# The last three steps of two attention layers, finished amid the weighing of the following step

## The reference: what is computed

```python
h = jnp.maximum(_layernorm(x, axis=-1), 0.0)
x = x + layer(h, adj, ...)
```

```python
Wh = jnp.einsum('nf,hfo->hno', node_features, W)
e = leaky_relu(f_src[:, :, None] + f_dst[:, None, :], 0.2)
attn = jax.nn.softmax(jnp.where(adj > 0, e, NEG_INF), axis=-1)
h_prime = jnp.einsum('hnm,hmo->hno', attn, Wh)
```

## Time and profile before

| | |
|---|---|
| median of three runs | 1111.23 us |
| the profiled execution, its own time | 1109.11 us |
| its span, first to last instruction | 1106.9 us |
| TensorE matmul busy | 844.4 us (76%) |
| VectorE busy | 774.2 us (70%) |
| ScalarE busy | 430.3 us (39%) |
| GpSimd busy | 634.1 us (57%) |
| mean granted TensorE clock | 0.906 |

### The profile page before, as it was taken

The page is one execution under the profiler, slowest core; times in us unless marked ns, Lnnn a source line. Parts: engine busy times, 40 slices in busy tenths (PEclk is TensorE's granted clock), DMA queues, the critical chain, the costliest instruction groups (busy, mean ns, idle before and its releaser), DMA issues. The chain is left out here.

```text
span 1106.9 us, 11271 instructions
## 1 busy us (share of the span) xinstructions
PE 844.4 (76%) x2786; PEld 471.1 (43%) x2786; DVE 774.2 (70%) x2327; ACT 430.3 (39%) x1277; POOL 634.1 (57%) x636
## 2 busy tenths in 40 slices
PE   0889869999928745959999989467799928876354
PEld 0344434433317534835666646244444523332121
DVE  3899986943349839938689995477899825646374
ACT  3677868111115423624554334355663511110000
POOL 5003401667767777437776730677777057777772
PEclk9999989999959986988999999898999959997767
DMA  9998998938878898647887841678778267776761
GB/s 358 413 395 336 386 393 251 324 104 267 267 248 285 284 233 284 202 153 214 246 245 209 227 128 47 177 232 239 222 211 229 72 155 205 203 206 196 199 189 73
DMA packets 87599, 257.49 MB, mean 233 GB/s; under 512 B 18694, under 2 KB 22182, under 8 KB 83433
## 3 DMA queue, kind: packets, MB, share of 16 engines
q0 software_dynamic: 46896, 157.18, 49.3%
q1 hardware_dynamic: 33116, 85.89, 21.1%
q10 hardware_dynamic: 7516, 13.63, 3.5%
HBM read 209.81 MB, written 53.66 MB: 238 GB/s over the span
## 5 line engine op out<-in xcount | busy, mean ns | idle before, releaser
L1148 POOL DMA_INDIRECT arena<-T,arena x476 | 497.7, 1046 | 266.5 <-issue 202.8
L771 PE MATMUL psum<-arena,misc 128*128 128x512 f32 x408 | 207.3, 630 | 32.9 <-DVE arena L1527 25.4
L747 PE MATMUL psum<-arena 128*128 128x264 f32 (+1 forms) x832 | 207.8, 394 | 0.9 <-ACT arena L869 0.9
L670 PE MATMUL psum<-misc,arena 128*128 128x128 f32 (+1 forms) x520 | 87.3, 294 | 153.6 <-ACT arena L853 93.0
L747 PEld LDWEIGHTS psum<-arena 128*128 128x128 f32 (+1 forms) x832 | 159.5, 195 | 59.3 <-issue 25.6
L1527 DVE TENSOR_TENSOR arena<-arena 128x512 f32<-128x512 f32 x238 | 157.4, 689 | 1.2
L670 PEld LDWEIGHTS psum<-misc,arena 128*128 128x128 f32 (+1 forms) x520 | 65.2, 150 | 198.3 <-ACT arena L853 109.5
L853 ACT ACTIVATE arena<-arena 128x512 f32<-128x512 f32 x104 | 85.0, 818 | 114.8 <-DVE arena L1405 70.0
L822 PE MATMUL psum<-arena 128*128 128x512 f32 (+1 forms) x208 | 110.3, 679 | 19.2 <-ACT arena L866 19.2
L771 PEld LDWEIGHTS psum<-arena,misc 128*128 128x128 f32 x408 | 75.4, 200 | 103.5 <-issue 66.8
L869 ACT ACTIVATE arena<-psum 128x128 f32<-128x128 f32 (+1 forms) x312 | 82.3, 283 | 88.8 <-PE psum L670 88.7
(11 more groups left out here) (143 smaller groups left out, 972.5 us busy)
## 6 DMA issues: line engine op xcount, KB each, us to landing
arena<-in_adj SPq DMA_DIRECT2D x25, 1663.5 KB, 12.4
T<-arena SPq DMA_DIRECT2D x75, 260.0 KB, 3.8
arena<-T,arena POOLq DMA_INDIRECT x476, 4.2
T<-arena ACTq DMA_DIRECT2D x25, 256.0 KB, 9.4
XV<-in_x SPq DMA_DIRECT2D x1, 6400.0 KB, 29.8
XV<-arena ACTq DMA_DIRECT2D x25, 256.0 KB, 3.8
PW<-arena POOLq DMA_DIRECT2D x5, 1024.0 KB, 27.0
arena<-in_x SPq DMA_DIRECT2D x1, 3072.0 KB, 18.7
```

The lines of the kernel that those rows point to most:

```text
L670: last = e.transpose(to[:, k * P:k * P + n], src[0:n, k * P:(k + 1) * P], ident[0:n, 0:n])
L747: last = e.matmul(p_wh[m % 2][0:n, a, :], ht[:, k, 0:n], WL[l][:, k, a, :], start=k == 0, stop=k == 3)
L771: e.matmul(p_num[s % 3].rearrange("p (a o) -> p a o", a=2), ident, halves(GB[:, BASE[l, s] + of[n][0], :])[:, :, 0:HALF], start=n == 0, st ...
L1148: e.indirect_dma_start(GB[:, BASE[l, s] + k, 0:ROW], None, dr["T"][l], bass.IndirectOffsetOnAxis(ap=(IDP if l else IDX)[:, t, k:k + 1], ax ...
```

## The change

The last three steps are 23, 24 and 25 (`LATE = NT - 3`). VectorE finishes step 23 in the middle of round 25 in place of the start of round 26, and step 24 in the middle of round 26 in place of round 27, each behind the third operation of `weigh`; step 25 comes in round 27 in place of 28. Ahead of it all that is left of the norm before it is emitted in one go. The rest of the norm of the step is spread over the rest of that round. On ScalarE `new_h` and `squares` of these steps stand in one block ahead of `exp`, `new_h` of a step first and `squares` of the step after it behind.

```diff
+    LATE = NT - 3
@@ scalar
         for l in (1, 2):
             for r in range(NT + 6):
-                if 0 <= r - 3 < NT:
+                if 0 <= r - 3 < LATE:
                     squares(l, r - 3)
...
+                if LATE <= r - 2:
+                    if 0 <= r - 3 < NT:
+                        new_h(l, r - 3)
+                    if r - 2 < NT:
+                        squares(l, r - 2)
                 if r < NT:
                     exp(l, r)
-                if 0 <= r - 3 < NT:
+                if 0 <= r - 3 < LATE - 1:
                     new_h(l, r - 3)
@@ vector
-            for r in range(NT + 3):
-                fin = finish(l, r - 3) if r >= 3 else none
-                nrm = norm(l, r - 3) if r >= 3 else none
+            for r in range(NT + 2):
+                on = 0 <= r - 1 < NT
+                done = NT - 1 if r == NT + 1 else r - 3 if 0 <= r - 3 < LATE else None
+                fin = none if done is None else finish(l, done)
+                nrm = none if done is None else norm(l, done)
...
                     if k:
                         go(nrm, 2)
                         go(sh)
+                    if LATE <= r - 2 < NT - 1 and k == SLOTS[ORDER[r - 1]] // 2 - 1:
+                        go(nrm, 12)
+                        go(finish(l, r - 2), 2)
+                        nrm = norm(l, r - 2)
```

More of the change, by code:

```diff
@@ L1562, in vector @@
         for l in (1, 2):
-            for r in range(NT + 3):
-                fin = finish(l, r - 3) if r >= 3 else none
-                nrm = norm(l, r - 3) if r >= 3 else none
+            for r in range(NT + 2):
[3 more added lines that the diff above has]
+                nrm = none if done is None else norm(l, done)
                 sh = shifted(l, r) if r < NT else none
-                on = 0 <= r - 1 < NT
                 nz = normalized(l, r - 1) if on else none
```

## The result

The changed kernel takes 1122.96 us, the median of four runs (1120.07 to 1125.82), and the kernel before 1110.88 us in four runs beside them (1106.15 to 1111.57). The ratio is 1.010, with a 95% interval of 1.0068 to 1.0133: slower, as forecast, by 12.1 us. The prediction was 1120 in a range from 1112 to 1127, and its sum 10.8 us. The profiled span is 1121.1 us.

A forecast was written before the change was run, and what follows sets the result against it. VectorE was taken to bound layer 1's rounds 25 and 26, while TensorE lagged 1.74 us in layer 2. Layer 1's 6.2, layer 2's 3.4 and the clock's 1.2 summed to 10.8 us more: 1120 us, range 1112 to 1127.

The forecast's parts named there:

- one finish and one norm more: Layer 1: VectorE does this extra work before its last weighing ends, 2.3 us.
- waits for squares: VectorE stalls for ScalarE's squares in rounds 25 and 26: 1.1 and 2.8 us in layer 1, 0.9 and 1.2 in layer 2.
- lower clock: Layer 1's rounds 25 and 26: TensorE's clock falls behind idle stretches, 0 to 2.4 us, one fall of 1.2 taken.
- sum after the lag: Layer 2: 5.1 us of VectorE work and stalls, of which TensorE's 1.7 us lag hides a part, leaving 3.4 us.
- shortening of the drains: Behind the last sum in both layers: finishing earlier gains nothing, distance to the next layer's first gather unchanged.
- What bounds the rounds: VectorE sets layer 1's rounds 25 and 26; layer 2's round 26 has TensorE without a gap, lagging by 1.74 us.
- The wait in round 26: Layer 1: late transposes of step 22 delay ScalarE's queue up to squares(24), so VectorE stalls 2.8 us.
- Covered and shorter: Both layers: TensorE's lag covers VectorE's extra work and the drain may shrink; 1105.6 us at best, or 1109; chance 0.14.
- Only the floor: Both layers: each stall is only 0.88 us and the clock holds; 7.2 us more, 1116 us; chance 0.20.
- costs more: Lower clock behind both layer 1 idle stretches, layer 2 stores landing in 4.2 us, not 2.1; 1125 us; chance 0.15.
- it doesn't do what it says: Round 25: the finish comes later than meant because step 23's sums aren't done; 1112 us; chance 0.01.
- One sign: Profile after the change: layer 2's first gather comes 6 to 9 us later.

The follow-up runs named there:

- waits_out: Changed kernel with two weighings between centred and the norm's rest, layer 1's squares(24) before node_ht(22), two zero products in round 25: 1113.88 against 1110.06 us, ratio 1.0031.
- kept_warm: Changed kernel with three zero-matrix products where TensorE would stand idle in layer 1's steps 24 and 25: 1237.12 against 1224.79 us, ratio 1.0121.
- layer1_only: Kernel before, with the early finish of steps 23 to 25 in layer 1 alone: 1119.75 against 1113.14 us, ratio 1.0053.
- own_buffers: Kernel before, with layer 2's rows of steps 24 and 25 in free gather ring places: ratio 1.0014, then in a second run 1108.82 against 1110.06 us, 0.9987.
- step24_only: Kernel before, with only step 24 finished early, in round 26, in both layers: 1115.93 against 1110.06 us, ratio 1.0039.
- squares_first: Changed kernel, with ScalarE doing squares(24) before node_ht(22) in layer 1's round 26: 1229.5 against 1224.79 us, ratio 1.0145.
- step23_only: Kernel before, with only step 23 finished early, in round 25, in both layers: 1116.07 against 1113.14 us, ratio 1.0027.
- layer2_only: Kernel before, with the early finish of steps 23 to 25 in layer 2 alone: 1115.0 against 1113.14 us, ratio 1.0029.

## Why the prediction was right, step by step

| D1, layer 1 | predicted | measured |
|---|---|---|
| one finish and one norm more | 2.3 | 2.0 (waits_out) |
| waits for squares | 1.1 + 2.8 | 1.07 + 3.10 in the profile; 3.85 in D1 (kept_warm less waits_out) |
| lower clock | 1.2 (0 to 2.4) | 1.64 and 4.21 in two executions |
| sum | 7.4 | 7.51 |
| D2, layer 2: waits | 0.9 + 1.2 | 0.97 + 1.39 |
| D2: sum after the lag | 3.4 | 3.43 |
| shortening of the drains | 0 | 0.00 and 0.02 |

The measured parts of D1 add up to 7.51 because they are the differences between four profiles in a row (before, waits_out, kept_warm, changed). How well the sum of 7.4 met the 7.51 is partly luck, since another execution of the same layer 1 had 10.08 (layer1_only). The forecast of 1120 was also put between two bases, the profiled execution (1119.9) and the median (1122.0); the medians moved by 12.1 us against the 10.8 forecast.

**What bounds the rounds.** Right in both layers. The drain after step 23's transposes kept its 16.53 us in every profile with layer 1's full change, and the distance from the last sum to the gather in layer 2 its 14.8. So an earlier finish had nothing to win there, as long as TensorE's products in layer 1 and the stores of rows 22 and 23 in layer 2 were next. own_buffers shows the second (an early finish together with free buffers wasn't run); that products hold layer 1's drain is read from TensorE's timeline alone, no run changed it.

**The wait in round 26.** The chain worked out, VectorE late, transposes late, node_ht, products_out, new_h, squares, gave 2.8 us and the trace has 3.10. step24_only and squares_first cut it in two places, and it fell to 0.94 and 0.88. My hand schedule left out that the finish itself would wait for TensorE (0.35 us).

**The clock.** The right mechanism and the wrong size of range: I had put 0 to 2.4 us and taken one fall; the clock fell twice, and one execution of the two profiled lost 4.21. The low clock outlasted the first unit behind the idle stretch and met the products behind it, and it wasn't made up in VectorE's waits. The Trainium skill, "TensorE: Matmul & The Clock Gate", Part 1, which the prediction named, says that the throttled state is the default and that activity releases it. The traces agree: the clock fell behind both idle stretches, and in kept_warm, with 2.74 us of products of zeros in each of them, it stayed at 1.00.

**The lag.** The sum of layer 2 was right, and luck had a part in it. VectorE's last weighing came 5.03 us later (5.1 predicted), of which 2.36 were waits (2.1) and 2.67 work (3.0), and the lag took 1.58 (1.7): two errors of 0.3 us cancel. The way of reckoning held only since both rounds had VectorE late by more than the lag. Where a round was relieved afterwards (step23_only, layer 2) the same reckoning gave 0 and the run 1.78 us.

**The rivals.** "Covered and shorter" is excluded by layer2_only for the layer in which it had a case. "Only the floor" needed both waits at 0.88 and a clock that holds; the floor itself exists, in squares_first and step24_only. Of "costs more" the one half came true, the lower clock behind both idle stretches; the other didn't: the stores in layer 2 took 2.1 us (876.93 to 879.05), not 4.2. The finish stood where it was meant to, so "it doesn't do what it says" is out. One sign was off by a little: layer 2's first gather came 9.2 us later and not 6 to 9, but 1.65 of that was there before layer 1's round 25. The 12.1 us between the medians are 1.2 more than D1 and D2 together, and inside what the medians of four runs leave open.

## What to carry to other kernels

Before an operation is moved ahead of other work, write down what each engine's queue holds between its signal and its answer; here a nine-operation norm was moved next to the operation it waits for, and close to 6 us of the 11 (3.85 in layer 1, 1.99 in layer 2) were the price of VectorE standing still for an answer that used to have cover. Cover is a stock: set the delay against the lag at that moment, not at the end of the stage, and treat what goes beyond it as lost on an engine without gaps. And look for what holds the stretch that is to be shortened first: a drain that is held by products or by a store doesn't get shorter by an earlier input.

## What the runs showed of the hardware

Two idle stretches of TensorE (3.40 and 3.16 us) cost D1 1.64 us in one profile and 4.21 us in another by the half clock behind them, with the same instructions and the same idleness, so single profiles of such a kernel can differ by 2.6 us in one stage. The store of a row took 2.12 and 2.13 us from the end of scores_out to the new_h that waited for it. The distances that the edits left alone repeat to 0.03 us, D1 even on a chip on which the whole kernel takes 10% longer (1224.79 against about 1111 us). Of the 129 us between the two profiles of own_buffers none lie in D1; 94 lie before layer 1's round 25, the rest in layer 2 and behind it, in stretches with gathers in them. Why that chip is slower there no run shows.
